# Rank features of the shared passes computed in four column tiles of the array

## What is computed

```
x = x + attention(layernorm(x), ctx, ctx, lengths)
t = layernorm(x)                                   # 2048 tokens x 512
shared = gelu(t @ sw1 + sb1) @ sw2 + sb2 + gelu(t @ swd) @ swu      # swd: 512 x 32, swu: 32 x 512
experts: top 2 of 8 per token, at most 320 tokens for each choice of an expert,
         y = gelu(b @ w1[e] + b1[e]) @ w2[e] + b2[e] + gelu(b @ wd[e]) @ wu[e]
out = x + sum over choices of weight * y + 0.2 * shared
```

## Time and profile before

| | |
|---|---|
| median of 3 runs | 1345.88 us (1344.07 to 1348.02) |
| the profiled execution | 1344.16 us, its span 1342.3 us |
| mean granted clock of the array | 0.993 |
| PE busy | 1295.6 us, 97% of the span |
| ACT, DVE, POOL busy | 708.8, 842.5, 256.1 us |
| the nine shared passes | begin between 73.7 and 598.5 us |
| the experts | from 644.9 us to the end |

### The profile page before, as it was taken

The page is one execution under the profiler, slowest core; times in us unless marked ns, Lnnn a source line. Parts: engine busy times, 40 slices in busy tenths (PEclk is TensorE's granted clock), DMA queues, the critical chain, the costliest instruction groups (busy, mean ns, idle before and its releaser), DMA issues.

```text
span 1342.3 us, 26800 instructions
## 1 busy us (share of the span) xinstructions
PE 1295.6 (97%) x10963; PEld 943.3 (70%) x11024; DVE 842.5 (63%) x1420; ACT 708.8 (53%) x1056; POOL 256.1 (19%) x219
## 2 busy tenths in 40 slices
PE   5888999999999999999999999999999999999997
PEld 2252736455564647385788889999999988888895
DVE  7776769697788887764652845638356283562730
ACT  4867676757676776672433534535345353442521
POOL 3750001000010041523300301203022030120012
PEclk9899999999999999999999999999999999999999
DMA  9615141423375233415736767677585775867413
GB/s 282 210 38 126 35 119 52 118 56 88 79 69 107 69 75 102 119 33 90 250 100 135 201 142 200 152 141 206 143 211 136 138 203 139 190 153 144 95 25 40
DMA packets 195627, 168.21 MB, mean 125 GB/s; under 512 B 117945, under 2 KB 138569, under 8 KB 195506
## 3 DMA queue, kind: packets, MB, share of 16 engines
q1 hardware_dynamic: 183218, 141.30, 40.8%
q0 software_dynamic: 12288, 25.21, 11.1%
HBM read 109.47 MB, written 34.15 MB: 107 GB/s over the span
## 4 chain that ended last, share of the span: by engine, by line
PE 86%; ACT 6%; DVE 4%; issue 3%; DMA 1%; SPq 0%; POOLq 0%; POOL 0%; another core or an unknown queue 0%; ACTq 0%; DVEq 0%
PE banks L1913 25%; PE banks L1943 24%; PE banks L1847 10%; PE banks L1829 10%; PE banks L1769 4%; PE banks L1749 3%; PE banks L1717 3%; ACT QS L1130 2%; ACT hidden L1143 2%; ACT hf L1189 1%; PE banks L1778 1%; PE banks L1803 1%; PE banks L1954 1%; PE banks L1815 1%; DVE rowmax L1371 1%
## 5 line engine op out<-in xcount | busy, mean ns | idle before, releaser
L1943 PE MATMUL banks<-hidden,w2h 128*128 128x0 bf16 x2048 | 306.1, 269 | 0.0
L1143 ACT ACTIVATE hidden<-banks,scales 128x512 f32<-128x512 f32 x256 | 171.0, 688 | 91.2 <-PE banks L1749 60.7
L1943 PEld LDWEIGHTS banks<-hidden,w2h 128*128 128x128 bf16 x2048 | 198.6, 98 | 20.5
L1371 DVE TENSOR_REDUCE rowmax<-banks 128x1 f32<-128x512 f32 x256 | 173.3, 686 | 35.1 <-PE banks L1717 33.6
L1943 PE MATMUL banks<-hidden,w2l 128*128 128x0 bf16 x1024 | 192.3, 269 | 0.0
L1522 DVE TENSOR_TENSOR w1l<-stage,w1h 128x2048 bf16<-128x2048 f32 x32 | 73.2, 2293 | 187.4 <-ACT w1h L1220 187.4
L1847 PE MATMUL banks<-w2h,hidden 128*128 128x512 bf16 x498 | 179.0, 379 | 1.4 <-DVE hidden L1506 0.6
L1237 ACT ACTIVATE hf<-banks,b1cols 128x640 f32<-128x640 f32 x128 | 101.5, 793 | 122.4 <-PE banks L1913 103.1
L1248 ACT ACTIVATE yT<-banks 128x640 uint16<-128x640 uint16 x56 | 36.4, 703 | 215.2 <-PE banks L1943 215.2
L1913 PE MATMUL banks<-eth,w1h 128*128 128x0 bf16 x1024 | 133.0, 273 | 0.0
L1913 PE MATMUL banks<-etl,w1h 128*128 128x0 bf16 x1024 | 132.9, 273 | 0.0
(11 more groups left out here) (199 smaller groups left out, 1966.8 us busy)
## 6 DMA issues: line engine op xcount, KB each, us to landing
stage<-in_L_ffn_w SPq DMA_DIRECT2D x64, 1024.0 KB
split_parts<-hidden SPq DMA_DIRECT2D x16, 512.0 KB, 4.7
QS<-split_parts SPq DMA_DIRECT2D x48, 128.0 KB, 2.7
KS<-split_parts SPq DMA_DIRECT2D x48, 128.0 KB, 3.2
xin<-in_x SPq DMA_DIRECT2D x16, 256.0 KB, 3.7
cin<-in_ctx SPq DMA_DIRECT2D x16, 256.0 KB, 3.9
out_rows<-xin SPq DMA_DIRECT2D x16, 256.0 KB, 2.0
normed_rows<-x2r SPq DMA_DIRECT2D x16, 256.0 KB, 3.3
```

The costliest lines, as they stand in the source:

```text
L1143: ac.activation(prob[n % NPH], bank(score_bank[unit]), ACT.Exp, scale=scales[:, g // 2:g // 2 + 1]).then_inc(s_exp, 1)
L1371: dv.reduce_max(rowmax[g % 2][:, i:i + 1], bank(score_bank[unit]), X_AXIS).then_inc(s_max, 1)
L1943: issued = mm(bank(b0 + j)[:, skips[j]:CAP].shape_from_register(used_cols(e, j)), w[:, fb, rows], of_choice(a[:, fb, :], j, skips[j]).shap ...
```

## The change

The unit `rank` gets the form that `e_rank` has. The 256 (or 128) tokens of a pass are taken in four quarters of 64 (32). Each quarter has its own 32 columns of the array, so the weights `wdh` and `wdl` have 32 columns, not three times 32. PE issues 48 matmuls in place of 12. ACT brings the four quarters together with four Gelus in place of one; the last raises `s_rgelu`. DVE casts twice in place of once and subtracts as before. The split of the shared rank weights is one cast and one subtraction in place of three and three.

```diff
-        wdh, wdl = sb("wdh", [P, KB, WIDE], BF16), sb("wdl", [P, KB, WIDE], BF16)
+        wdh, wdl = sb("wdh", [P, KB, RANK], BF16), sb("wdl", [P, KB, RANK], BF16)
...
-        lowf = sb("lowf", [WIDE, SLOTS], F32)
+        lowf = sb("lowf", [RANK, SLOTS], F32)
...
                     w = P * len(groups_of(p))
-                    ac.activation(lowf[:, 0:w], bank(b)[0:WIDE, 0:w], ACT.Gelu).then_inc(s_rgelu, 1)
+                    q = w // RANK_TILES
+                    for c in range(RANK_TILES):
+                        issued = ac.activation(lowf[0:RANK, c * q:(c + 1) * q], bank(b)[c * RANK:(c + 1) * RANK, 0:q], ACT.Gelu)
+                    issued.then_inc(s_rgelu, 1)
...
-                    copies = 3 if e == E else 1
-                    for j in range(copies):
-                        link(dv.tensor_copy(wdh[:, :, j * RANK:(j + 1) * RANK], wdf[:, :, :]))
+                    link(dv.tensor_copy(wdh[:, :, :], wdf[:, :, :]))
                     dve.wait_ge(s_dve, chain)
-                    for j in range(copies):
-                        issued = dv.tensor_tensor(wdl[:, :, j * RANK:(j + 1) * RANK], wdf[:, :, :],
-                                                  wdh[:, :, j * RANK:(j + 1) * RANK], ALU.subtract)
-                        if j == copies - 1:
-                            issued.then_inc(s_wdc, 1)
+                    dv.tensor_tensor(wdl[:, :, :], wdf[:, :, :], wdh[:, :, :], ALU.subtract).then_inc(s_wdc, 1)
...
-                    if kind == "rank":
-                        w = P * len(groups_of(m))
-                        link(dv.tensor_copy(o[0:WIDE, 0:w], lowf[:, 0:w]))
-                        dve.wait_ge(s_dve, chain)
-                        dv.tensor_tensor(o[HD:2 * HD, 0:w], lowf[HD:2 * HD, 0:w], o[HD:2 * HD, 0:w],
-                                         ALU.subtract).then_inc(s_low, 1)
-                    else:
-                        link(dv.tensor_copy(o[0:RANK, :], lowf[0:RANK, :]))
-                        link(dv.tensor_copy(o[2 * RANK:3 * RANK, :], lowf[0:RANK, :]))
-                        dve.wait_ge(s_dve, chain)
-                        dv.tensor_tensor(o[RANK:2 * RANK, :], lowf[0:RANK, :], o[0:RANK, :], ALU.subtract).then_inc(s_low, 1)
+                    w = P * len(groups_of(m)) if kind == "rank" else SLOTS
+                    link(dv.tensor_copy(o[0:RANK, 0:w], lowf[0:RANK, 0:w]))
+                    link(dv.tensor_copy(o[2 * RANK:3 * RANK, 0:w], lowf[0:RANK, 0:w]))
+                    dve.wait_ge(s_dve, chain)
+                    dv.tensor_tensor(o[RANK:2 * RANK, 0:w], lowf[0:RANK, 0:w], o[0:RANK, 0:w], ALU.subtract).then_inc(s_low, 1)
...
                     n = 0
+                    q = w // RANK_TILES
                     for weights, data in ((wdh, xth[p % 2]), (wdh, xtl[p % 2]), (wdl, xth[p % 2])):
                         for kb in range(KB):
                             n += 1
-                            issued = mm(bank(b)[0:WIDE, 0:w], weights[:, kb, :], data[:, kb, 0:w], start=n == 1, stop=n == 3 * KB)
+                            for c in range(RANK_TILES):
+                                issued = mm(bank(b)[c * RANK:(c + 1) * RANK, 0:q], weights[:, kb, :],
+                                            data[:, kb, c * q:(c + 1) * q], start=n == 1, stop=n == 3 * KB)
```

## The result

The changed kernel takes 1348.51 us, median of 20 runs (1344.84 to 1353.55); the kernel before, beside it on the same chip, 1343.92 us, median of 20 (1339.44 to 1348.02). The ratio is 1.0032, with a 95% interval of 1.0021 to 1.0043: slower by some 4.3 us (2.8 to 5.8). The forecast was 1349.4 us, from +3.5 us. The profiled execution took 1345.78 us, with a span of 1344.0.

What follows compares the result with a forecast made beforehand. Though the array is busy 97%, it waits for ACT's and DVE's rank work. Split -0.7, pass 0 +1.1, pass 1 +0.4, passes 2 to 6 +2.1, pass 7 +0.6: +3.5 us on median 1345.88, 1349.4 us; range 1343 to 1353.5.

Steps and rivals of the forecast that it cites:

- The array's part: Rank matmuls in passes 1 to 7: 0.56 us for 1.31, a gain of 0.75 us in each.
- ACT's part: Rank Gelu of a 256-token pass: four small Gelus take 0.9 us, 0.5 more than the one now.
- DVE's part: Rank casts and subtraction: begin 0.33 us late, second cast 0.31 us more, everything behind on DVE 0.64 us later.
- Who is late next: Passes 2 to 6: the later sum of exponentials uses up 0.2 us of slack before L1778, +0.43 us each, 2.1 in all.
- The first of the two waits: Passes 2 to 6: second hidden block waits for the Gelu's bank, so at most 0.14 us of the 0.75 arrive.
- Pass 7: DVE's work after the Gelu is 0.83 us later, so the array waits for the sum of exponentials: +0.5 to 0.6 us.
- Pass 0: DVE's third rank operation takes one more turn beside GpSimd's subtractions: +1.1 us (0.6 to 1.6), array idle some 2.4 us.
- Weight split: Shared rank weights at 46 us: two casts and two subtractions fewer on DVE, -0.7 us (bounds 0 and -1.3).
- The sum: All terms over the whole kernel: +3.5 us on the profiled execution, 1349.4 us on the median of the runs.
- (A): Rival, all passes: the waits are looser and the array's gain arrives, 6.2 us faster, 1339.7 us; chance 0.10.
- (B): Rival, pass 0: array idle past 2 us brings a clock drop costing 3 us more, 1352.4 us; chance 0.22.
- (C): Rival, near 54 us: DVE sooner by 0.7 us shortens the half-speed stretch by 3 us, 1346.4 us; chance 0.10.

Runs made afterwards that it cites:

- e1: Kernel before with its one rank Gelu cut into four by columns and a second DVE cast, matmuls and tripled weights kept; ratio 1.0021 to the kernel before.
- e5: Kernel before with two DVE casts and four 32x64 Gelus moving data to partitions 0 to 31, its 12 matmuls kept; ratio 1.0043 to the kernel before.
- e2: Changed kernel with one Gelu, one cast and one subtraction, using only the first quarter's rank features; ratio 0.9985 to the kernel before.
- e6: Changed kernel with DVE's two casts and subtraction of the rank unit queued later, ahead of the third hidden block's; ratio 0.9994 to the kernel before.
- e12: Changed kernel run and profiled once more, nothing altered; ratio 1.0029 to the kernel before.
- e8: Changed kernel with the shared rank weights split by three casts and three subtractions again, matmuls using the first copy; ratio 1.0046 to the kernel before.
- e4: Kernel before with only its one rank Gelu cut into four by columns (96x64 each); ratio 0.9991 to the kernel before.
- e10: Kernel before with DVE's one cast and subtraction of the rank unit moved later; ratio 0.9992 to the kernel before.
- e3: Kernel before with DVE's second cast alone added; ratio 1.0002 to the kernel before.

## Why the prediction was right

**The array's part: right.** 48 matmuls in 0.49 us and 0.09 for entering the tiled form make 0.58 against 0.56 forecast, 0.73 net for 0.75. On average they start 10 ns apart: the four of a round 3 to 4 ns, the rounds 29 ns and, in the last third, up to 35. The rule of 25 ns that the prediction weighed (the Trainium skill, TensorE: Matmul & The Clock Gate, "Wait — 56ns, not 53.3ns?") would have made them 1.2 us. Between neighbouring column tiles it does not hold; within one tile the trace agrees with it: in pass 0, with 32 columns each, matmuls on the same tile start 25 ns apart at the least.

**ACT's part: right.** 0.90 us forecast and measured in passes of 256 tokens, 0.79 in pass 0. What the estimate did not contain is its reason (e1 against e5): a Gelu of this size is not dear (0.21 us), but the four don't overlap, where e1's do. e1's have 96 rows that stay in their partitions, e5's have 32 that are moved to 0 to 31; which of the two matters no run separates.

**DVE's part: right.** The second cast comes 0.31 us behind the first (213.20, 213.51), as estimated. The row maximum begins 2.02 us behind the table load's end, 1.38 before: 0.64 late, the forecast's number.

**Who is late next: the size right, the wait misnamed.** The prediction took the 0.25 us between the sum's end and L1778 for the slack that decides, +0.43. What binds is one step earlier: the score after the second hidden block waits for the row maximum. Before, that maximum ended at 216.49 and the score began at 216.82, 0.33 us of slack; late by 0.64, with 0.05 for the hand-over, it gives 0.36, and 0.37 was measured. The two rows, of the timeline before:

```profile
215.80 0.69 DVE L1371 TENSOR_REDUCE rowmax<-banks 128x1 f32<-128x512 f32 x1
...
216.82 0.38 PE L1717 MATMUL banks<-KS,QS 96*128 96x512 bf16 x1
```

I had found this very wait in pass 1 and not looked for it in passes 2 to 6. Ones times the sum then begins 0.12 us behind the sum and 1.20 behind the score, as before, so it waits for nothing. In e2 both waits bind: the row maximum leaves 0.27 us of gain at the score, the sum 0.2. Both waits end the same path, so either name gives nearly the same sum: 5 times 0.43 was 2.1 us, measured 1.8.

**The first of the two waits** (L1823 for the Gelu) was priced right, with "at most 0.14 us of the 0.75 reach it". It takes 0.59 of the 0.73 us, and e6 shows it: with DVE cured, 0.12 us of gain is all that passes it. Only the expectation of e6 misread it, from the idle of 0.43.

**Pass 7: the size right, the wait misnamed.** +0.58 for 0.6. The prediction let the sum bind. But here the second hidden block waits longest, for the Gelus:

```profile
575.59 0.61 PE L1823 MATMUL banks<-xth,w1h 128*128 128x256 bf16 x4 [1.08 <-ACT lowf L1179]
```

It begins 0.97 us behind the table load's end, 0.45 before. e6, where DVE's part is out of the way, still has +0.51, so ACT's part makes nearly all of it.

**Pass 0**: +1.11 for 1.1, idle 2.46 for 2.4, by the mechanism forecast, in the first trace; in e12 +1.05 by another, with 1.54 us of idle, so of two traces one bears the forecast out.

**Weight split**: -0.5 for -0.7; DVE's L1328 begins 0.76 us behind the first cast (2.10 before), so 1.3 us sooner as worked out, and the operation that then falls under GpSimd (L1362, now L1365) takes 1.53 us for 0.68, a toll of 0.85 us, not 0.6.

**The sum.** With measured terms: -0.5 + 1.1 + 2.75 = +3.35 us, for +3.5 forecast (split -0.5 for -0.7, passes 1 to 7 2.75 for 3.1: the misses partly cancel), against 4.3 (2.8 to 5.8) measured in whole runs and 3.9 (2.0 to 5.8) in e12. The two agree within the intervals. The pass 0 term is the least sure: from the last exponential ahead of pass 0 to the one ahead of pass 1 the two traces of the changed kernel are +0.39 and +1.30 longer than the trace before, so part of the +1.1 is won back behind it. Whether the 1 us that the terms leave is there at all is open; if it is, pass 0 at its dear price in part of the runs would be one cause. For that speaks that e8 and the changed kernel, 2.8 us apart in pass 0 by their profiles, are apart by 0.14% or 1.9 us in whole runs, with intervals that overlap. Whole runs have no times by pass, so this was not settled. That 1348.51 lies within 1 us of the forecast 1349.4 is partly luck: the forecast stands on a median of 1345.88, 2.0 us above the one measured beside the changed kernel, and its +3.5 is 1.1 us short of the 4.6 us between the two medians.

**The rivals.** (A) fell: e5 shows that passes 1 to 7 don't feel the array at all. (B) is a real mechanism, with its point wrong: 2 us of idle was given as the point from which it decides, and as the idle forecast was 2.4 us, (B) should by its own words have been the forecast. 2.46 us left the clock at 1.00; 2.91 and more were followed by half clock, but so was 2.24 in e6. Idle time alone does not tell the cases apart, and what does is open. Its size, 3 us, was too large: 1.6 to 1.7 us were lost. (C) came in part. The stretch of 10.2 us at 54.6 us was one of 3.4 at 53.6 in the profile after, but e4 and e10, with the split of before, have 3.4 too. So I took all fourteen traces and the time from the split (47.8 us) to the last exponential ahead of pass 0, less that of before: the eight with tripled weights lie from -1.1 to +1.2, mean +0.3, the six with the smaller split from -1.6 to -0.2, mean -0.9. That is 1.2 us sooner, of which 0.5 are the split's own; some 0.7 us would be (C), for 3 forecast. The two groups overlap, and the traces of the changed kernel alone give -1.6 and -0.2, so its size stays open.

## What to carry to other kernels

Ahead of making matmuls faster, find the first operation behind them that another engine starts late anyhow, here the Gelu behind a table load of 1.28 us, and cost the whole path from it: if the array waits for that path, cheaper matmuls buy nothing, and what gathers their output is paid as far as it exceeds the slack (0.64 us late against 0.33 of slack here). Splitting the tokens over column tiles paid here only with the gathering where nothing of the pass hangs on it, and even then less than half (0.34 of 0.82 us). To compare small edits, difference the traces over short fixed steps: the same kernel twice gave 0.00 us there and differed by 4 us in its span. Look at the rows too: in pass 0 two traces agreed within 0.06 us by different causes.

## What the runs showed of the hardware

- **Gelus overlap or don't.** Four of 96x64 that write the partitions they read start 0.105 us apart (0.56 in all, one lasts 0.22, e2). Four of 32x64 that bring data to partitions 0 to 31 start 0.225 apart (0.90 in all; after, e5). Whether the move or the 32 rows do it is open.
- **A fill by GpSimd holds up a DVE cast, and not a subtraction.** The cast lasts the whole 1.83 us of the fill (e1, e5, e8); the subtraction of the same 32x128 takes its bare 0.28 us under the same fill (e3, e12, e5). GpSimd's subtractions hold up both, for 1.1 us each. The Trainium skill (SBUF — State Buffer, "Terms") was cited for the lock; these rows agree for the cast, and show that not every operation of DVE is held.
- **Column tiles**: 48 matmuls of 64 columns in 0.49 us. On neighbouring tiles they start 3 to 4 ns apart, on the same tile 29 ns and more, and with 32 columns 25 ns (pass 0). Entering the tiled form costs another 0.09 us.
- **Half clock after an idle**: idles of 2.24 us (e6) and of 2.91 to 3.2 us (e1, e5, e8) were followed within 0.8 us by 3.4 us at 0.50, one of 2.46 us (the changed kernel) was not.
- **An idle that the rows show for PE can be too short**: 0.43 us shown, 0.59 by the starts.
